# Gated linear attention in chunks of 64 tokens in place of 128, with two chunks side by side in the matrix engine

## The reference

```python
H = 8; DK = 128; DV = 32; GATE_NORM = 16.0
q = (x @ Wq).reshape(B, S, H, DK)
k = (x @ Wk).reshape(B, S, H, DK) * DK ** (-0.5)
v = (x @ Wv).reshape(B, S, H, DV)
alpha = jax.nn.sigmoid((x @ Wg + bg) / GATE_NORM)      # one gate per token and head
def step(state, inp):
    qt, kt, vt, at = inp
    state = at[..., None, None] * state + kt[..., None] * vt[:, :, None, :]
    out_t = jnp.einsum('bhk,bhkv->bhv', qt, state)
    return (state, out_t)
_, outs = lax.scan(step, state0, xs)
og = jax.nn.sigmoid(x @ Wog)
return out * og @ Wo
```

## Time and profile before

| what | value |
|---|---|
| time, median of 3 runs | 538.67 us (536.96 to 538.70) |
| span of the profiled execution | 534.6 us; the page gives no other time for it |
| PE busy | 507.4 us (95%), 3304 matmul records |
| DVE, ACT, POOL busy | 388.8 (73%), 327.2 (61%), 170.4 us (32%) |
| attention steps | about 249 to 430 us |
| one step in the middle | 24.16 us: PE 24.16, DVE 20.11, ACT 12.52, POOL 11.14 us busy |

### The profile page before, as it was taken

One profiled execution on the slowest core, in us unless ns is written; L12 is line 12 of the kernel. 1 busy time (PEld: TensorE's weight loads), 2 busy tenths in 40 slices (PEclk: granted clock), 3 DMA queues, 4 the chain that ended last, 5 costly groups with the idle time before them and its releaser, 6 DMA issues.

```text
span 534.6 us, 9257 instructions
## 1 busy us (share of the span) xinstructions
PE 507.4 (95%) x3304; PEld 392.7 (73%) x3304; DVE 388.8 (73%) x1020; ACT 327.2 (61%) x599; POOL 170.4 (32%) x241
## 2 busy tenths in 40 slices
PE   8599989998999999989899999999999989999995
PEld 6568877786687878868567777767677668888884
DVE  6986987698768785646989888887979864554433
ACT  4978968686867788846364454646454444555541
POOL 3510640033003002101425254534536364343311
PEclk9869999999999999998999999999999999999998
DMA  8500000000003000004343332323333100000101
GB/s 307 176 1 1 2 0 1 1 2 1 0 1 121 22 2 0 2 0 159 112 147 101 130 113 80 110 83 110 103 113 116 50 1 2 21 21 23 38 20 40
DMA packets 18607, 31.15 MB, mean 58 GB/s; under 512 B 2400, under 2 KB 13152, under 8 KB 18432
## 3 DMA queue, kind: packets, MB, share of 16 engines
q1 hardware_dynamic: 17504, 30.00, 17.4%
q10 hardware_dynamic: 1056, 0.52, 0.3%
HBM read 28.19 MB, written 2.33 MB: 57 GB/s over the span
## 4 chain that ended last, share of the span: by engine, by line
PE 46%; ACT 3%; DMA 2%; DVE 1%; SPq 1%; issue 1%; POOL 1%; POOLq 0%; ACTq 0%
PE bank L1929 10%; PE bank L2010 6%; PE bank L165 5%; PE bank L167 5%; PE bank L166 5%; PE bank L1941 3%; PE bank L1975 3%; PE bank L1963 2%; PE bank L241 2%; PE bank L2002 1%; PE bank L1950 1%; ACT att_qT L1766 1%; DMA cum_rows<-att_cum 1%; PE bank L2018 1%; ACT h_hi L247 1%; DMA att_prob<-cut_rows 1%
## 5 line engine op out<-in xcount | busy, mean ns | idle before, releaser
L1066 PE MATMUL bank<-ffn_g_hi,w_hi 128*128 128x512 f32 x288 | 116.7, 405 | 0.1
L1067 PE MATMUL bank<-ffn_g_lo,w_hi 128*128 128x512 f32 x288 | 114.0, 396 | 0.0
L607 DVE TENSOR_TENSOR ffn_g_lo<-ffn_full,ffn_g_hi 128x512 fp32r<-128x512 f32 x96 | 67.1, 699 | 27.2 <-ACT ffn_full L853 25.8
L1414 DVE TENSOR_TENSOR_SCAN att_prob<-att_prob,bank 128x512 f32<-128x512 f32 x64 | 77.0, 1208 | 7.5 <-DMA att_prob<-cut_rows 7.4
L1929 PE MATMUL bank<-att_qT,h_full 128*128 128x512 f32 x128 | 67.3, 610 | 1.3 <-DVE att_prob L1425 1.3
L1793 ACT COPY att_qT<-bank 128x512 f32<-128x512 f32 x64 | 36.6, 583 | 46.0 <-PE bank L167 43.1
L1066 PEld LDWEIGHTS bank<-ffn_g_hi,w_hi 128*128 128x128 f32 x288 | 54.3, 188 | 13.8 <-issue 1.7
L1067 PEld LDWEIGHTS bank<-ffn_g_lo,w_hi 128*128 128x128 f32 x288 | 54.3, 189 | 11.7
L853 ACT ACTIVATE ffn_full<-bank,cols 128x512 f32<-128x512 f32 x64 | 44.2, 696 | 20.8 <-PE bank L1067 14.5
L1425 DVE TENSOR_TENSOR att_prob<-bank,att_prob 128x512 f32<-128x512 f32 x64 | 43.2, 676 | 18.9 <-PE bank L1929 18.7
L1607 POOL TENSOR_TENSOR att_vw<-att_v,att_prob 128x128 f32<-128x128 f32 x64 | 26.1, 408 | 92.1 <-DVE att_prob L1414 92.1
(11 more groups left out here) (230 smaller groups left out, 1137.8 us busy)
## 6 DMA issues: line engine op xcount, KB each, us to landing
att_prob<-cut_rows SPq DMA_DIRECT2D x32, 512.0 KB, 4.7
att_wide<-cum_rows SPq DMA_DIRECT2D x64, 48.0 KB, 1.9
out<-att_vw SPq DMA_DIRECT2D x7, 256.0 KB, 2.3
x<-in_x SPq DMA_DIRECT2D x3, 512.0 KB, 12.1
w_raw<-in_w_all SPq DMA_DIRECT2D x1, 1152.0 KB, 8.4
w_raw<-in_w_all SPq DMA_DIRECT2D x1, 768.0 KB, 9.6
v_raw<-in_v_all SPq DMA_DIRECT2D x1, 576.0 KB, 5.9
x<-in_x ACTq DMA_DIRECT2D x2, 256.0 KB, 3.5
```

The lines of the kernel that those rows point to most:

```text
L607: dve.tensor_tensor(lo, full[j % 4][:, :], hi.bitcast(F32), ALU.subtract).then_inc(low, 1)
L1066: pe.matmul(acc, w[0], x[0], start=start, stop=False)
L1067: return pe.matmul(acc, w[0], x[1], start=False, stop=stop)
L1414: dve.tensor_tensor_scan(w, w, eyes[:, :], 0.0, ALU.mult, ALU.add).then_inc(decay_ready, 1)
```

## The change

Chunks have 64 tokens in place of 128. Tiles of decays hold two chunks above each other, the even chunks on partitions 0 to 63, the odd ones on 64 to 127, and are half as wide: two heads fit into one scan of 512 columns. `score` handles four chunks of four heads into one bank with four products of 64 x 256; the even chunk writes partitions 0 to 63, the odd one 64 to 127, so that each takes half the columns of the array. `inside` has products with 64 rows (the tokens of one chunk), even chunks into one bank and odd ones into another. There are seven chained states in place of three, from products with 64 rows in four banks, and `cross` runs for seven chunks of 64 tokens. The gates go to DRAM in two transfers a sequence, and each spreading transfer is cut in two of a quarter of the bytes.

```diff
@@ attention_lora
+C = P // 2
+NC = S // C
+Q = S // 2
-    LEAD = PER
+    LEAD = 2
+    PAIRS = NH // 2
+    LATE = NC - 1
+    STATE_BANK = (0, 1, 0, 1, 3, 2, 3)
+    STATE_SLOT = (0, 0, 1, 1, 0, 0, 1)
+    STATE_FREE = (3, 4, 6, 7)
...
-        prob = [sb(f"att_prob{m}", [P, PER, S]) for m in range(KEEP)]
+        prob = [sb(f"att_prob{m}", [P, PER, Q]) for m in range(KEEP)]
...
-                uses.append(("score", b, k))
+                if k % 2 == 0:
+                    uses.append(("score", b, k // 2))
                 if k == 0:
-                    uses += [("inside", b - 1, 1)] * p + [("og", b, 0), ("og", b, 1)] + [("alpha", b + 1, 0)] * n
+                    uses += [("inside", b - 1, 2), ("inside", b - 1, 3)] * p + [("og", b, 0), ("og", b, 1)] + [("alpha", b + 1, 0)] * n
...
-                    uses.append(("inside", b, 0))
+                    uses += [("inside", b, 0), ("inside", b, 1)]
                 if k == 6:
-                    uses += [("state", b, 0), ("state", b, 1)]
+                    uses += [("state", b, q) for q in range(4)]
...
+                def scan(b, j):
+
+                    n, q = b * GROUPS + j // 2, j % 2
+                    dve.wait_ge(spread_in[n % KEEP][q], 32 * (n // KEEP + 1))
...
+                    w = prob[n % KEEP][:, 2 * q:2 * q + 2, :].rearrange("p e n -> p (e n)")
                     dve.tensor_tensor_scan(w, w, eyes[:, :], 0.0, ALU.mult, ALU.add).then_inc(decay_ready, 1)
...
                 def states(b):
                     s = b % 2
-                    for c in range(3):
+                    for m in range(LATE):
...
                     for k in range(NH):
-                        if b * NH + k + LEAD < B * NH:
-                            scan(*divmod(b * NH + k + LEAD, NH))
-                        weigh(b, k)
+                        if k % 2 == 0:
+                            ahead = b * PAIRS + k // 2 + LEAD
+                            if ahead < B * PAIRS:
+                                scan(*divmod(ahead, PAIRS))
+                            weigh(b, k // 2)
...
                     for q in range(2):
-                        heads = r["cut_rows"][b, g * PER + 2 * q:g * PER + 2 * q + 2, :]
-                        sp.dma_start(prob[n % KEEP][:, 2 * q:2 * q + 2, :], over(heads, 0, [P, 2, S])).then_inc(spread_in[n % KEEP][q], 16)
+                        for u in range(2):
+                            heads = r["cut_rows"][b, g * PER + 2 * q:g * PER + 2 * q + 2, u, :]
+                            sp.dma_start(prob[n % KEEP][half_rows(u), 2 * q:2 * q + 2, :], over(heads, 0, [C, 2, Q])).then_inc(spread_in[n % KEEP][q], 16)
...
+                def score(b, j):
+                    ps = claim(pe, "score", b, j)[:, :].rearrange("p (e t n) -> p e t n", e=PER, n=C)
+                    for t in range(2):
+                        for u in range(2):
+                            at = (2 * half + t) * P + u * C
+                            mm = pe.matmul(ps[half_rows(u), :, t, :], hT[s][:, at:at + C], qT[s][:, heads, at:at + C], start=True, stop=True)
...
                 def inside(b, g):
+                    ps = [claim(pe, "inside", b, 2 * g + u) for u in range(2)]
+                    for t in range(T):
+                        for u in range(2):
+                            for e in range(PER):
+                                k = g * PER + e
+                                mm = pe.matmul(ps[u][e * DV:(e + 1) * DV, t * C:(t + 1) * C], v[s][half_rows(u), t, k * DV:(k + 1) * DV], group(b, k)[half_rows(u), e, t * C:(t + 1) * C], start=True, stop=True)
...
                 def states(b):
+                    ps = [claim(pe, "state", b, q) for q in range(4)]
+                    for m in range(LATE):
+                        t, u = m // 2, m % 2
+                        at = STATE_SLOT[m] * HV
+                        mm = pe.matmul(ps[STATE_BANK[m]][:, at:at + HV], htok[s][half_rows(u), t, :], vw[s][half_rows(u), t, :], start=True, stop=True)
+                        if m in (2, 3, 5, 6):
+                            mm.then_inc(ring_mm, 1)
```

More of the change, by code:

```diff
@@ L1323, in attention_lora @@
         USES = [(use, n % RING) for n, use in enumerate(ATT_USES)]
-        USES.insert(ATT_USES.index(("score", LAST, 5)), (("down", 0, 0), RING))
+        USES.insert(ATT_USES.index(("inside", LAST, 0)), (("down", 0, 0), RING))
         USES += lora_uses()
@@ L1350, in __call__ @@
                         "q": (q_ready, b * NH + k + 1),
[L1351 removed]
+                        "score": (prob_ready, b * PAIRS + k + 1), "og": (og_ready, 2 * b + k + 1),
                         "htok": (htok_ready, b + 1), "total": (total_ready, b + 1),
[L1353 removed]
+                        "inside": (inner_ready, 4 * b + k + 1), "state": (state_ready, LATE * b + (STATE_FREE[k] if what == "state" else 0)),
                         "cross": (outer_ready, 2 * b + k + 1), "y": (added, b + 1),
@@ L1646, in finish @@
                     pool.tensor_tensor(res[s][:, 0:ts, :], r["x"][:, b, 0:ts, :], upd[s][:, 0:ts, :], ALU.add).then_inc(res_ready, 1)
-                for k in range(LEAD):
+                for k in range(2 * LEAD):
                     decay_v(0, k)
@@ L1734, in normalise @@
                     if b == B + 1:
-                        act.wait_ge(ring_mm, full("state", LAST - 1, 1))
+                        act.wait_ge(ring_mm, full("state", LAST - 1, 3))
                     elif b > B + 1:
@@ L1815, in keep_inner @@
                         act.wait_ge(gated, b - 1)
-                    act.wait_ge(ring_mm, full("inside", b, g))
-                    act.copy(inner[b % 2][:, g, :], bank("inside", b, g)[:, :]).then_inc(inner_ready, 1)
+                    for u in range(2):
+                        act.wait_ge(ring_mm, full("inside", b, 2 * g + u))
+                        src = bank("inside", b, 2 * g + u)[:, 0:Q].rearrange("p (t n) -> p t n", n=C)
+                        act.copy(half_of(inner[b % 2][:, g, :], u), src).then_inc(inner_ready, 1)
                 act.activation(table[:, :], r["neg_half"][:, :], ACT.Sigmoid)
@@ L1921, in rest @@
                     ps = claim(pe, "total", b, 0)
-                    pe.matmul(ps[:, 0:T * NH], r["ones"][:, :], ends[s][:, :, :].rearrange("p c n -> p (c n)"), start=True, stop=True).then_inc(ring_mm, 1)
-                def score(b, k):
-                    s, c, heads = b % 2, k % T, slice(k // PER * PER, (k // PER + 1) * PER)
+                    pe.matmul(ps[:, 0:NC * NH], r["ones"][:, :], ends[s][:, :, :].rearrange("p c n -> p (c n)"), start=True, stop=True).then_inc(ring_mm, 1)
+                def score(b, j):
+                    s, g, half = b % 2, j // 2, j % 2
+                    heads = slice(g * PER, (g + 1) * PER)
                     pe.wait_ge(q_ready, b * NH + heads.stop)
-                    ps = by_chunk(claim(pe, "score", b, k)[:, :])
-                    pe.matmul(ps, hT[s][:, c * P:(c + 1) * P], qT[s][:, heads, c * P:(c + 1) * P], start=True, stop=True).then_inc(ring_mm, 1)
+                    ps = claim(pe, "score", b, j)[:, :].rearrange("p (e t n) -> p e t n", e=PER, n=C)
+                    for t in range(2):
+                        for u in range(2):
+                            at = (2 * half + t) * P + u * C
+                            mm = pe.matmul(ps[half_rows(u), :, t, :], hT[s][:, at:at + C], qT[s][:, heads, at:at + C], start=True, stop=True)
+                    mm.then_inc(ring_mm, 1)
                 def inside(b, g):
@@ L1947, in states @@
                     pe.wait_ge(vw_ready, (b + 1) * NH)
-                    ps = claim(pe, "state", b, 0)
-                    for c in range(2):
-                        mm = pe.matmul(ps[:, c * HV:(c + 1) * HV], htok[s][:, c, :], vw[s][:, c, :], start=True, stop=True)
-                    mm.then_inc(ring_mm, 1)
-                    ps = claim(pe, "state", b, 1)
-                    pe.matmul(ps[:, 0:HV], htok[s][:, 2, :], vw[s][:, 2, :], start=True, stop=True).then_inc(ring_mm, 1)
+                    ps = [claim(pe, "state", b, q) for q in range(4)]
[4 more added lines that the diff above has]
+                        if m in (2, 3, 5, 6):
+                            mm.then_inc(ring_mm, 1)
                 def cross(b):
```

129 lines of the change are left out of this document (64 added, 65 removed).

## The result

| | before | changed |
|---|---|---|
| time, median (lowest to highest) | 538.24 us (536.96 to 538.70) | 557.40 us (553.36 to 561.12) |
| profiled execution: time, span | span 534.6 us | 553.36 us, span 551.4 us |
| mean granted clock of TensorE | 0.980 | 0.969 (0.954 in the runs of 561.12 and 560.58) |
| ratio to before | 1 | 1.0371, 95% interval 1.0335 to 1.0408 |

The changed kernel is 3.7% slower by the ratio in the table; the two medians divided give 1.0356, inside its interval. The forecast was 529.5 us, 1.7% faster.

What follows compares the result with a forecast made beforehand. PE was taken as the bound: a step of 24.16 us becomes 21.80 of PE work plus 1.19 of wait, 22.99. Together -9.2 us, span 525.4, time 529.5 us; forecast's own range 526 to 533, wider range 520 to 541.

Steps and rivals of the forecast that it cites:

- What PE puts out: PE's own work in an attention step, without waits: 21.80 us after the change, 2.36 less than before.
- Score group: Four score products into one bank on PE: two rounds, 0.86 us, replacing two scores; four groups 3.45 a step.
- states: State products on PE: seven products in four rounds of two records, 1.72 us (+0.42), or 3.01 without overlap.
- rival (d): Score products on PE: halves of columns don't overlap, +3.45 us a step, step 25.2, time 546; chance 4%.
- rival (a): Inside and states on PE: halves of rows don't overlap, step 24.0 us, time 537.4; chance 15%.
- inside: Inside products on PE: 32 products twice, 16 rounds if halves of rows overlap, 0.90 us a step (-0.84).
- Rival (c): Short records on PE cost their slot whatever their width: 0.027 us each, step 25.9, time 550; chance 11%.
- 0.99 for each pair: DVE's serial chain of states: 0.99 us for each pair of instructions, seven states ending 6.36 us after the copy's start.
- what I don't see: Chance of 9% for unseen effects, such as POOL and DVE in each other's way during the longer chain.
- what hides the rest: the transfer: DVE's scan: its transfer, with a wait of 0.75 us before, has half the bytes and DVE comes 3 us later.
- the price of a wait: PE's waits in each step counted at their length: 1.19 us added to 21.80, giving a step of 22.99.
- 4.1 us from span to time: Whole kernel: median of the runs 4.1 us over the profiled span, so a span of 525.4 gives 529.5 us.

Runs made afterwards that it cites:

- the order of 528.35 us: Changed kernel with the gate ahead of the states, low_h held back, state products 4 to 6 behind k=7's queries and DVE's add first: 528.35 us, ratio 0.9830.
- the experiment that keeps POOL away: Changed kernel with both edits: low_h waiting for the seven states, join and gate moved ahead of them: 536.55 us, ratio 0.9985.
- gate early: Changed kernel with DVE's next scan behind across and POOL's join and gate ahead of the decays of k=4: 538.39 us, ratio 1.0031.
- `low_h` late: Changed kernel with POOL's low_h waiting until the seven states of the step before are done: 548.28 us, ratio 1.0214.
- split: Changed kernel with PE issuing state products 4 to 6 behind the queries of k=7: 544.73 us, ratio 1.0140.
- split and add first: Changed kernel with state products 4 to 6 behind k=7's queries and DVE's add ahead of scan and weigh at k=0: 535.81 us, ratio 0.9977.

## Why the prediction was wrong

**What PE puts out: right in kind, 0.55 us too low.** The step is 22.35 us of PE, 21.80 priced. Some 0.2 of it are tails of records that end in a wait; in the order of 528.35 us, where PE does not wait, the step is 22.50 with one more change of the division, priced at 0.35. Score group 1.01 with its entry (0.86 + 0.15), cross 1.71 (1.57 and the entry), states 1.92 (1.72 + 0.2) came as priced. Halves of columns overlap, or a group would take 1.7; so rival (d) is out. Halves of rows overlap, or the states would take over 3.0; rival (a) is out. The Trainium skill ("TensorE: Matmul & The Clock Gate", Part 3) has products in distinct row groups run at once; these rows agree, with 1.92 for seven products. The mis-sized term is inside: its 64 records take 0.80 from start to start where 0.45 and a share of the entering and leaving (some 0.13) were priced, 0.0125 us a record. Rival (c), 0.027 a record, would have made it 1.75 and cross 3.06. Twice some 0.2, and the tails, make about the 0.55.

**The step that failed: "0.99 for each pair".** It was read from a stretch of the kernel before in which POOL had nothing to do with SBUF: its gate had ended 0.25 us ahead of the copy. In the changed kernel the chain is three times as long and reaches to `low_h`, and the gate is not over when it begins: it ends 1.67 us behind the copy's start (345.87 for 344.20), beside the first product. Two stops of 1.0 and 0.86 us made 6.36 into 8.19. I had left this to the 9% of "what I don't see", without a price. In the experiment that keeps POOL away the term is as priced, 6.40. That the wait is as priced too, 1.21 for 1.19, is in part luck: priced were 0.85 at the inside products and 0.34 ahead of the gate logits for `add`, and measured is all of it at the inside products, because the copy comes 0.3 us later in that order. Ahead of the gate logits PE waited in no middle step of the changed kernel.

The Trainium skill ("SBUF — State Buffer", Who interferes with whom) has the rule I should have weighed: a DVE instruction with two SBUF inputs and a GpSimd instruction that reads SBUF exclude each other for the whole instruction, and the one that starts first wins. The rows read here agree. `att_grown` (two SBUF inputs) ends behind gate or `low_h`; `att_state` (one input in PSUM) takes 0.42 in all 48 instances, also while `low_h` runs; two scans over `bank`, whose second input is in PSUM, take 2.32 us together beside a gate, while the scan of `cumulate` over two SBUF tiles makes the join 2.88; and `low_h`, started second, takes 1.49.

**The second step that failed: "what hides the rest: the transfer".** I argued it for the second half of the heads alone, and there it held. For the first half DVE, which has half its scans left, comes 3 us sooner after the gates' save, and SP issues four transfers in place of two. It waits 2.53 us, in step 0 5.71; the prediction had let PE's wait of 1.33 us in step 0 go, and it became 3.23. The claim that `across`, join and gate have room was right for the output products, which did not wait in the middle steps; ahead of those of the last step PE waited 2.90 us, before 1.15, where -0.1 was priced. But I asked only who waits for the gate, not what runs beside it. That cost the most: the order that undoes it is worth 19.0 us alone. This figure takes in the waits of the scan, those of step 0 and both collisions of the middle steps, which no run takes apart further.

**The third: the price of a wait.** The sum took a wait at its length. Here five waits, of 2.69 and 3.23 us, were each followed by a stretch at 1.2 GHz worth about 1.7 us more, 8.5 us in the attention and 6.4 net over the kernel. The runs of 561 us differ from that of 553 by the clock (0.954 for 0.969; 0.015 of 559 is 8.4 us); where in those runs it fell, no trace shows.

Together, for the step from 352.53: 22.99 priced, + 0.55 PE, + 1.7 wait (2.9 for 1.19), + 1.5 clock = 26.7, measured 26.73. The prediction had named 24.2 as the bound above which it is wrong.

**The last term, 4.1 us from span to time, was too high.** It set the median of three runs against the span of one. Every execution for which both numbers are known took 1.8 to 2.1 us more than its own span. This would have lowered the forecast by 2 us and explains nothing of the miss.

**What each cause is worth.** The edits are not additive, because each changes when `low_h` and the gate meet the chain and which claim waits for it: gate early 19.0 us, `low_h` late 9.1, both 20.9; split 12.7, split and add first 21.6; all of them 29.1. The fastest order takes 528.35 us, 1.7% less than before, with a step of 22.50 for 24.16. That this is the percentage of the forecast is luck. The forecast had a chain of 6.4 us and a wait of 1.2 in each step, and the kernel with those rows, POOL kept away, takes 536.55 us, no difference to before. The gain of 1.7% comes only with two edits that the forecast did not have, and which take PE's wait away, although PE's work in a step is above its price. Between the worst and the best order lie 5.4 points (1.0371 less 0.9830). Whether the kernel before would gain from the same edits was not tried; its PE waits 2.8 us in the attention altogether, which leaves it little to gain there.

## What to carry to other kernels

When a change lengthens a serial chain on DVE, lay POOL's timeline beside it as it will be, and price each product with two SBUF inputs at POOL's end, not at its own length; an operand in PSUM avoids it. Ask of every late instruction on an in-order queue what it delays into overlap, not only who waits for it. Give the banks that come free last to the user that comes last, and count a PE wait as long as these (2.7 us, in some cases 1.9) as itself plus a possible 1.7 us of lower clock.

## What was not expected of the hardware

- 32 products of 64 rows by 32 columns, 64 records, take 0.80 us from start to start, 12.5 ns a record, below the 25 ns at which records of one tile follow each other.
- 14 us of additional products filled PE's waits and the kernel became 0.9% faster relative to before (1.0279 for 1.0371, in different sessions).
- A product of 128x64 that takes 0.23 us alone took 1.93 beside POOL's join, and the join 2.88 in place of 2.10 beside a scan over two SBUF tiles: the sizes of the two no longer tell their times.
